# Moving VectorE's side work of a step from behind the minimum to between the maximum and the minimum of the score tiles

## The reference, cut to what matters

```python
embedded = emb_table[src]; h = embedded @ W_e2h + b_e2h
for i in range(6):                      # gated convolutions, kernel size 3
    a, g = split(conv(x, conv_w[i]) + conv_b[i]);  x = (a * sigmoid(g) + x) * SCALE
h = x.T @ W_h2e + b_h2e;  n = layernorm(h)
attn1 = softmax(q1 @ k1.T * scale);  attn2 = softmax(q2 @ k2.T * scale)   # 8 heads each, 1024 x 1024
# mean, std, max and min of the rows of both, averaged over windows of 4 rows:
alpha = sigmoid(mlp(concat(stats(attn1), stats(attn2))))
h = h + ((alpha * attn1 + (1 - alpha) * attn2) @ v) @ Wo
h = h + moe(layernorm(h))               # fc1, gelu, fc2, next, gelu
```

## Time and profile before

| | |
|---|---|
| median of 3 runs | 5982.09 us (5976.68 to 5983.98) |
| the profiled execution | 5978.36 us, its span 5975.9 us |
| busy share of the span | PE 87%, ACT 87%, DVE 86%, POOL 41% |
| mean granted TensorE clock | 0.955 of full speed |

### The profile page before, as it was taken

One profiled execution on the slowest core, in us unless ns is written; L12 is line 12 of the kernel. 1 busy time (PEld: TensorE's weight loads), 2 busy tenths in 40 slices (PEclk: granted clock), 3 DMA queues, 4 the chain that ended last, 5 costly groups with the idle time before them and its releaser, 6 DMA issues.

```text
span 5975.9 us, 121038 instructions
## 1 busy us (share of the span) xinstructions
PE 5203.4 (87%) x34070; PEld 2503.5 (42%) x34070; DVE 5115.8 (86%) x7715; ACT 5221.3 (87%) x7937; POOL 2454.1 (41%) x4439
## 2 busy tenths in 40 slices
PE   6988989889898988989889898988889899898985
PEld 4443434444343443434334343443434344343443
DVE  2989899898998989899898988989899898988982
ACT  2999989899898989989889898989989899898984
POOL 6525344252433525344352433525344352533423
PEclk8999999999999999999999999999999999999997
DMA  1001010010101001010010101001010010101000
GB/s 37 20 23 27 17 31 20 21 27 23 27 19 29 20 21 27 19 31 19 21 28 23 27 19 29 20 21 27 20 31 18 22 28 21 27 20 29 19 22 12
DMA packets 164933, 140.87 MB, mean 24 GB/s; under 512 B 89196, under 2 KB 108268, under 8 KB 164140
## 3 DMA queue, kind: packets, MB, share of 16 engines
q1 hardware_dynamic: 159100, 124.09, 9.0%
q0 software_dynamic: 4352, 8.92, 0.7%
q10 hardware_dynamic: 816, 0.02, 0.0%
HBM read 21.26 MB, written 8.91 MB: 5 GB/s over the span
## 4 chain that ended last, share of the span: by engine, by line
PE 44%; issue 18%; DVE 15%; ACT 11%; POOL 8%; SPq 1%; DMA 1%; DVEq 1%; ACTq 1%; POOLq 1%
PE ps_w L389 19%; PE ps_t L389 10%; PE ps_o L389 9%; DVE neg_s L715 7%; PE ps_s L389 6%; DVE rowmin L723 4%; ACT exps L586 3%; ACT junk L579 3%; DVE bn L735 1%; SPq L330 1%; DVE o_raw L731 1%; POOL part L866 1%; POOL ctmp L986 1%; POOL ctmp L998 1%; ACT hpre L635 1%
## 5 line engine op out<-in xcount | busy, mean ns | idle before, releaser
L715 DVE TENSOR_SCALAR_CACHE_REDUCE neg_s<-ps_s 128x1024 f32<-128x1024 f32 x2048 | 2487.5, 1215 | 599.3 <-PE ps_s L389 526.2
L723 DVE TENSOR_REDUCE rowmin<-neg_s 128x1 f32<-128x1024 f32 x2049 | 2489.5, 1215 | 0.0
L579 ACT ACTIVATE junk<-neg_s,negmax 128x1024 bf16<-128x1024 f32 x2048 | 2353.0, 1149 | 149.4 <-DVE neg_s L715 145.1
L586 ACT ACTIVATE exps<-ps_t 128x1024 f32<-128x1024 f32 x2060 | 2110.6, 1025 | 255.6 <-PE ps_t L389 252.7
L389 PE MATMUL ps_t<-qst,kst 99*128 99x512 bf16 x4120 | 1293.3, 397 | 367.5 <-ACT exps L586 364.1
L389 PE MATMUL ps_o<-exps,v_cur 128*32 128x256 f32 x16512 | 1360.8, 402 | 272.6 <-DVE o_raw L731 240.7
L389 PE MATMUL ps_s<-kst,qst 96*128 96x512 bf16 x4096 | 1260.4, 389 | 44.1 <-DMA kst<-part 35.8
L389 PE MATMUL ps_w<-xc,cw 128*128 128x256 f32 x4704 | 1185.3, 388 | 1.0
L389 PEld LDWEIGHTS ps_w<-xc,cw 128*128 128x128 f32 x4704 | 914.7, 195 | 223.3 <-ACT chan L590 8.9
L389 PEld LDWEIGHTS ps_o<-exps,v_cur 128*32 128x32 f32 x16512 | 330.1, 109 | 1198.1 <-issue 643.9
L866 POOL TENSOR_SCALAR ctmp<-ug 128x256 f32<-128x256 f32 x408 | 165.8, 406 | 1554.7 <-ACT ug L655 1533.0
(11 more groups left out here) (181 smaller groups left out, 4025.1 us busy)
## 6 DMA issues: line engine op xcount, KB each, us to landing
qst<-part SPq DMA_DIRECT2D x1542, 32.0 KB, 2.0
kst<-part SPq DMA_DIRECT2D x1542, 32.0 KB, 2.0
qst<-mrow SPq DMA_DIRECT2D x1028, 1.5 KB
out_dram<-z SPq DMA_DIRECT2D x17, 512.0 KB, 3.2
fc1s<-in_fc_w SPq DMA_DIRECT2D x17, 256.0 KB
fc2s<-in_fc_w SPq DMA_DIRECT2D x17, 256.0 KB
cw<-in_conv_w SPq DMA_DIRECT2D x1, 2304.0 KB
odif<-in_table,idx POOLq DMA_INDIRECT x136
```

The source lines that it names most:

```text
L579: nc.scalar.activation(junk[:, n % 2, :], neg_s[:, n % SLOTS_S, :], ACT.Exp, scale=-1.0, bias=negmax[:, r, t:t + 1], accum_out=sumsq[:, r, ...
L586: nc.scalar.activation(exps[:, n % RING, :], ps_t[:, :, :].rearrange("p c q -> p (c q)"), ACT.Exp, scale=0.5).then_inc(s_exp, 1)
L715: nc.vector.tensor_scalar(neg_s[:, n % SLOTS_S, :], ps_s[:, n % 2, :], -1.0, None, ALU.mult, ALU.min, accum_out=negmax[:, r, t:t + 1]).the ...
L723: nc.vector.tensor_reduce(rowmin[:, r, t:t + 1], neg_s[:, m % SLOTS_S, :], axis=AX, op=ALU.max, negate=True).then_inc(s_min, 1)
```

## The change

The call of `row_min` moves behind the loop over the side tasks. Nothing is added or removed, and the streams of the four other engines stay as they were.

```diff
                     for n in range(STEPS):
                         row_max(i, n)
-                        row_min(i, n)
                         for tk in STEP[n]:
                             task("body", i, tk)
+                        row_min(i, n)
```

## The result

The changed kernel takes 5947.12 us (median of 4 runs, 5943.04 to 5952.66), the kernel before, run beside it, 5980.35 us (4 runs, 5976.68 to 5983.98). The ratio is 0.9945 with a 95% interval of 0.9928 to 0.9962: faster by 33 us. The profiled execution took 5952.66 us, its span 5950.7 us, and its mean granted TensorE clock is 0.947 of full speed against 0.955 before.

What follows compares the result with a forecast made beforehand. The bound was taken to change along a sequence among TensorE, VectorE and ScalarE, with the minimum delaying transposes TensorE awaits. Gains 3.43 minus losses 1.0 gave 2.43 us per sequence, times 16 = 39 us: 5939 us, range 5895 to 5995.

Steps and rivals of the forecast that it cites:

- Steps 57 to 80 and 54: Where TensorE sets the pace, its waits for `ps_o` go, plus one wait in step 54: gain 1.65 us per sequence.
- Steps 110 to 112: Behind the moments of `ln1`, TensorE starts 1.13 us earlier and VectorE's waits of 0.74 and 0.18 vanish: gain 0.92.
- h2e: Step 103: the wait for TensorE's matmuls loses the minimum's cover, 0.86, less 0.46 given back: net loss 0.40 us per sequence.
- I take nothing, with this as cover: Steps 23 to 27, `win`, `hid1`, `hid2`: VectorE's 1.5 us of score waits absorb added waits; cost nothing, 2.9 if cover goes.
- Steps 46 to 48: TensorE's wait of 0.86 goes and the scores of step 48 come 0.86 earlier: gain 0.86 us per sequence.
- `mrow` in step 8: Waits 1.08 us for GpSimd, up to 1.13 added; score waits up to step 15 take most: loss 0.2.
- `mrow` in step 120: Waits 1.26 us, 1.13 added, partly offset by earlier GpSimd work and free waiting: loss 0.3 us per sequence.
- `mrow` in other steps: Inputs come about 0.1 us after the maximum; loss of 0.1 us per sequence in all, together with `next`.
- next: Its input comes about 0.1 us after the maximum; counted within a loss of 0.1 us per sequence in all.
- Rival 1: Slower: waits the minimum covered stand open, 5.7 against gains of 3.43 per sequence, 36 us, 6014 us; chance 0.16.
- Rival 2: No change: TensorE's wait for ScalarE's exponentials replaces that for `ps_o`; 5978 us, give or take 12; chance 0.16.
- Rival 3: More: VectorE's score waits of 0.74 go in about 11 places, losses absorbed; 8 per sequence, 130 us, 5848 us; chance 0.10.

Runs made afterwards that it cites:

- the four transposes: Against the kernel before, only the transposes of `ps_o` of steps 53, 61, 69 and 77 moved in front of the minimum: 5953.26 us, ratio 0.9949.
- the units and the three gate tasks: Against the kernel before, the transposes of `ps_o` and `win`, `hid1`, `hid2` moved in front of the minimum: 5891.31 us, ratio 0.9859.
- the units: Against the kernel before, only the transposes of `ps_o` (task unit) moved in front of the minimum: 5888.30 us, ratio 0.9851.
- unit_mrow: Against the kernel before, the transposes of `ps_o` and all sixteen `mrow` tasks moved in front of the minimum: 5925.80 us, ratio 0.9909.

## Why the prediction was right, and where it was not

The sign, the kind of cause and the size hold: 5947.12 against 5939. But the sum was closer than its parts, because gains and losses were both set too small: 3.43 us per sequence of gains where the transposes alone bring 5.52, and 1.0 of losses where the other tasks alone cost 5.03. That the two errors cancelled was luck.

**Right in place and size.** Steps 57 to 80 and 54: 1.65 forecast, 1.95 measured, and shown alone by the four transposes. Steps 110 to 112: 0.92 against 1.14. The 0.18 us that the sum counts as a wait for scores is marked as issue in the earlier trace rows, and it stands in front of the maximum of step 112 after the change too (5073.28); the gain is 0.80 in step 110 and 0.33 in step 111 in the mean. There TensorE still waits 3.25 us (about 4 was said) and its eight matmuls still take 1.08 us at the low clock, with the scores in time all the same, timeline after, against the earlier trace rows:

```profile
5067.52 1.08 PE L389 MATMUL ps_o<-exps,v_cur 128*32 128x256 f32 x8 [3.25 <-DVE o_raw L731]
```

`h2e`: 0.40 lost against 0.37; `wo`: nothing against 0.11, in both as a gain of the transposes (0.54 and 0.70) that the open waits more than use up. The overlap cost of a side task behind a maximum was taken as 0, and the transpose starts 1.15 us behind its maximum, as the minimum did.

**The step that failed: "I take nothing, with this as cover" in the gate.** The cover itself held beside the earlier transposes: with the units and the three gate tasks the stretch is no longer. What the step did not see is that the earlier transpose of step 21 changes TensorE's clock. ScalarE's exponentials did not come earlier with it, so the same idle time fell into one wait of 1.9 us ahead of the sparse `win` matmuls, and the clock then ran at its lower level for some steps in 11 of 16 sequences instead of 5. That is 1.28 us per sequence, 20 us in all; two experiments took it away or brought it back by moving one transpose, or `snap` with the `mrow` ahead of it, with the clock going along each time. The clock itself was not set independently. That it is the cause and not a companion rests on the 16 sequences of the changed kernel's trace, which run the same program with the same two waits and lose time only where the clock fell, and on the matmuls of unchanged work that take 2.77 instead of 1.46 us there. Why it falls in one sequence and not in the next stays open.

**Mis-sized terms.**

- Steps 46 to 48: 0.86 forecast, 0.11 measured. TensorE's wait of 0.86 is gone, yet steps 44 and 48 are 0.24 and 0.26 us longer. With the units and `snap` the full 0.94 came; in that kernel the granted clock of steps 44 to 49 is 1.00 in every sequence, with the whole change 0.92 or 0.93 in 5 of 16. Those five take 23.30 us for steps 42 to 49, the others 21.6 to 22.0, and the kernel before 22.33. The 0.55 us that the earlier trace rows mark with GpSimd's `xc` were rightly read as a wait for scores: TensorE writes these from 4912.84 to 4913.44, and the maximum starts at 4913.55. So the term was right, and two things took it back: the clock, and the early `mrow` of step 48, with which `unit_mrow` has the same 0.25 us more in that step.
- `mrow` in step 8: 0.2 lost forecast; the later steps gave more than that back, 0.29 gained.
- `mrow` in step 120: 0.3 against 0.39, as a loss of 1.0 on a gain of 0.6 in step 118 and around it.
- `mrow` in other steps was put at 0.1 together with `next`; `unit_mrow` loses 0.64 in step 40, 0.26 in step 48 and 0.34 in step 104 by it.
- `next`: booked as part of a 0.1 loss, it is a gain of 0.6 to 0.9 over steps 81 to 99 (the whole change, and units with `next`, each against the units), in part by the clock.

**The rivals.** Rival 1 (open waits) is real: without the transposes it alone makes the kernel 91 us slower, 5.0 us per sequence, of which only 0.8 lie in the gate (1.7 in steps 116 to 127, 0.9 in 100 to 108, 0.8 in 35 to 41). Rival 2 holds in part: TensorE's wait for `exps` grew by 73 us, but not from step 57 to 80. Rival 3's gain is there in part as well: the transposes alone bring 5.5 us per sequence, between the 3.4 and the 8 of the text. Of the signs named beforehand, `o_raw` under 100 us was missed by 12, and the maximum of step 71 waits 0.27 rather than not at all; VectorE's waits for scores fell by 127 us where some 100 were told, and the open waits came at 0.85 to 2.40 us where 1 to 2 were told, except `win` with 3.06.

The Trainium skill ("TensorE: Matmul & The Clock Gate", Part 1) says that the clock follows how busy the engine has been of late. The traces agree in so far as the low clock in the rows shown stands behind a wait of TensorE (1.89, 5.08 and 3.25 us); that the same 2.5 us of idle time lowers it in 29 of 96 sequences or in 31 of 48, by how it is divided, only these runs show.

## What to carry to other kernels

On an engine that works its stream in order, put first what another engine waits for and whose input is ready, and leave work that needs no one (here the minimum) in front of tasks that themselves have to wait: moving only the transposes and `next` gave 0.982, moving all tasks 0.9945, and moving all but the transposes 1.015. Price the two kinds apart before adding them, since a fair sum can hide two terms that are each too small. Where an earlier start only turns two short waits of TensorE into one longer wait, read the granted clock behind it before booking the gain. Where a trace repeats the same work, sort the repetitions by their granted clock and compare like with like: the gate looked 1.28 us longer, and was 0.30 shorter at the full clock.

## What was unexpected of the hardware

The granted clock was 0.62 and 0.53 in the mean of the two stretches of 4 us behind a wait of 1.89 us (windows after), with TensorE busy throughout both; the division 0.6 and 1.9 us lowered it in 31 of 48 sequences, 1.5 and 1.0 us in the same steps in 29 of 96. The sixteen matmuls of 32 columns behind the wait took 1.57 and 1.84 us in the two timelines with a fall and 1.12 us in the two without. The same trace holds sequences with and without the fall behind equal waits, so the length of a wait alone does not decide it.
